# Bias and residual of an output chunk added by one VectorE instruction out of PSUM, in place of a ScalarE copy and a GpSimd addition

## What is computed

```python
q = split_heads(x @ Wq.T)
k, v = split_heads(text @ Wk.T), split_heads(text @ Wv.T)
k_ip, v_ip = split_heads(ip @ Wk_ip.T), split_heads(ip @ Wv_ip.T)
out = merge_heads(attend(q, k, v)) + merge_heads(attend(q, k_ip, v_ip))
return (out @ Wo.T + bo) + x
```

## Time and profile before

| | us |
|---|---|
| median of 3 runs | 683.67 (683.13 to 684.17) |
| the profiled execution | 683.04 |
| its span, first to last instruction | 681.2 |

### The profile page before, as it was taken

One profiled execution on the slowest core, in us unless ns is written; L12 is line 12 of the kernel. 1 busy time (PEld: TensorE's weight loads), 2 busy tenths in 40 slices (PEclk: granted clock), 3 DMA queues, 4 the chain that ended last, 5 costly groups with the idle time before them and its releaser, 6 DMA issues.

```text
span 681.2 us, 18904 instructions
## 1 busy us (share of the span) xinstructions
PE 657.5 (97%) x6514; PEld 564.5 (83%) x6514; DVE 435.7 (64%) x956; ACT 493.3 (72%) x1078; POOL 225.0 (33%) x261
## 2 busy tenths in 40 slices
PE   9959798999999999999999999999999999999997
PEld 9959576788888888888888888888888888888877
DVE  6786677675757566675756576665657566756633
ACT  3983787877868777877777787778777777876730
POOL 4020102243432434343434324343434243342333
PEclk9989898999999999999999999999999999999999
DMA  8950111223131221313131312213131323212212
GB/s 318 410 234 9 25 56 34 80 57 96 49 103 51 82 63 55 93 48 97 51 93 49 99 55 86 55 55 93 48 101 51 90 55 93 56 50 64 56 42 69
DMA packets 34691, 57.46 MB, mean 84 GB/s; under 512 B 4832, under 2 KB 27232, under 8 KB 34400
## 3 DMA queue, kind: packets, MB, share of 16 engines
q1 hardware_dynamic: 34656, 56.99, 27.3%
HBM read 35.34 MB, written 10.49 MB: 67 GB/s over the span
## 4 chain that ended last, share of the span: by engine, by line
PE 85%; DVE 6%; ACT 6%; issue 2%; POOL 0%; DVEq 0%; ACTq 0%
PE q_ps L711 19%; PE x_ps L711 19%; PE sum_ps L769 11%; PE b_ps L752 10%; PE pv_ps L780 10%; PE a_ps L735 7%; PE x_ps L789 5%; PE a_ps L741 1%; ACT probs L405 1%; DVE k_stack L631 1%; DVE k_stack L641 1%; ACT k_stack L485 1%; ACT q_stack L397 1%; DVE wo_lo L554 1%; DVE k_stack L545 1%
## 5 line engine op out<-in xcount | busy, mean ns | idle before, releaser
L405 ACT ACTIVATE probs<-b_ps 77x512 f32<-77x512 f32 x320 | 181.1, 591 | 121.0 <-PE b_ps L752 119.3
L562 DVE TENSOR_TENSOR q_stack<-q_ps,q_hi 32x256 fp32r<-32x256 f32 x320 | 134.3, 420 | 36.0 <-ACT q_hi L390 32.3
L571 DVE TENSOR_REDUCE row_max<-a_ps 128x4 f32<-128x308 f32 x320 | 137.6, 471 | 24.0 <-PE a_ps L735 21.3
L397 ACT ACTIVATE q_stack<-q_hi 32x256 fp32r<-32x256 f32 x320 | 133.0, 416 | 10.0
L598 DVE TENSOR_TENSOR scaled<-x_ps,pv_sb 128x512 f32<-128x512 f32 x75 | 51.9, 692 | 105.4 <-PE x_ps L789 105.0
L752 PE MATMUL b_ps<-q_stack,k_stack 98*77 98x256 f32 x640 | 115.1, 281 | 0.5 <-ACT probs L405 0.5
L347 POOL TENSOR_TENSOR scaled<-scaled 128x256 f32<-128x256 f32 x80 | 59.2, 740 | 139.1 <-DVE scaled L598 139.0
L352 POOL TENSOR_TENSOR attn_lo<-scaled,attn_hi 128x256 fp32r<-128x256 f32 x80 | 59.1, 739 | 113.2 <-ACT attn_hi L434 113.2
L358 POOL TENSOR_TENSOR res<-y,res 128x256 f32<-128x256 f32 x70 | 51.1, 731 | 136.8 <-ACT y L428 136.8
L735 PE MATMUL a_ps<-k_diag,q_hi 128*128 128x308 f32 x320 | 87.3, 313 | 7.0 <-DVE row_max L571 6.8
L752 PEld LDWEIGHTS b_ps<-q_stack,k_stack 98*77 98x77 f32 x640 | 85.7, 146 | 1.5 <-ACT probs L405 1.0
(11 more groups left out here) (111 smaller groups left out, 962.3 us busy)
## 6 DMA issues: line engine op xcount, KB each, us to landing
x_raw<-x_in SPq DMA_DIRECT2D x16, 640.0 KB, 4.2
q_stack<-q_stack SPq DMA_DIRECT2D x80, 128.0 KB, 2.3
res<-x_in SPq DMA_DIRECT2D x75, 128.0 KB, 2.0
y_out<-res SPq DMA_DIRECT2D x75, 128.0 KB, 1.7
stage<-wk_in SPq DMA_DIRECT2D x6, 640.0 KB, 7.9
stage<-wv_in SPq DMA_DIRECT2D x6, 640.0 KB, 10.7
wq_raw<-wq_in SPq DMA_DIRECT2D x1, 1600.0 KB, 10.2
wo_raw<-wo_in SPq DMA_DIRECT2D x1, 1600.0 KB, 14.6
```

The lines of the kernel that those rows point to most:

```text
L397: done = nc.scalar.activation(q_stack[0:D, u.slot, j, :], q_hi[j * D:(j + 1) * D, u.slot, :].bitcast(F32), ACT.Copy)
L405: nc.scalar.activation(probs[0:KEYS, j, :], b_ps[j % 2][0:KEYS, :], ACT.Exp).then_inc(b_drained, 1)
L562: done = nc.vector.tensor_tensor(q_stack[D:2 * D, u.slot, j, :], q_ps[rows, 0:N], q_hi[rows, u.slot, :].bitcast(F32), ALU.subtract)
L571: nc.vector.tensor_reduce(row_max[:, u.slot, br, :, sub], bank[:, 0:BLK].rearrange("p (j n) -> p j n", j=GROUP), AXIS.X, ALU.max).then_inc ...
```

## The change

The ScalarE copy `add_bias` with its buffer `y`, the GpSimd addition `add_residual` and the semaphore `y_added` are taken out. DVE gets a function `finish`, one `scalar_tensor_tensor` that reads the chunk out of `x_ps`, adds the bias as a scalar of each partition and the residual, and writes `res`. It signals `y_done`, for which PE's `spread_inverse` and now SP's `store` wait. In DVE's `emit` it stands behind `q_low`.

```diff
-        y = sbuf("y", [P, 2, N])
...
-        y_added = sem("y_added")
...
             def store(c):
-                wait(sp, y_added, c.number(1, 1))
+                wait(sp, y_done, c.number(1, 1))
...
-            def add_residual(c):
-                wait(pool, y_done, c.number(1, 1))
-                wait(pool, res_loaded[c.g], c.tile(DMA, DMA))
-                nc.gpsimd.tensor_tensor(res[:, c.g, :], y[:, c.slot, :], res[:, c.g, :], ALU.add).then_inc(y_added, 1)
...
-                if chunk.exists():
-                    add_residual(chunk)
...
-            def add_bias(c):
-                wait(act, out_ready, c.number(1, 1))
-                nc.scalar.activation(y[:, c.slot, :], x_ps[:, 0:N], ACT.Identity, bias=bo[:, c.g:c.g + 1]).then_inc(y_done, 1)
...
-                if chunk.exists():
-                    add_bias(chunk)
...
+            def finish(c):
+                wait(dve, out_ready, c.number(1, 1))
+                wait(dve, res_loaded[c.g], c.tile(DMA, DMA))
+                nc.vector.scalar_tensor_tensor(out=res[:, c.g, :], in0=x_ps[:, 0:N], scalar=bo[:, c.g:c.g + 1],
+                                               in1=res[:, c.g, :], op0=ALU.add, op1=ALU.add).then_inc(y_done, 1)
...
                 if u.plus(2).exists():
                     q_low(u.plus(2))
+                if chunk.exists():
+                    finish(chunk)
```

More of the change, by code:

```diff
@@ L353, in attn_low @@
                                         attn_hi[:, u.batch, u.g, :].bitcast(F32), ALU.subtract).then_inc(attn_lo_done, 1)
-            def add_residual(c):
-                wait(pool, y_done, c.number(1, 1))
-                wait(pool, res_loaded[c.g], c.tile(DMA, DMA))
-                nc.gpsimd.tensor_tensor(res[:, c.g, :], y[:, c.slot, :], res[:, c.g, :], ALU.add).then_inc(y_added, 1)
             def emit(u):
-                ahead, norm, chunk = u.tile_plus(1), u.plus(-1 - SPREAD_LAG), u.plus(-OUT_LAG)
+                ahead, norm = u.tile_plus(1), u.plus(-1 - SPREAD_LAG)
                 if norm.exists():
@@ L437, in emit @@
                 before, ahead, nxt = u.tile_plus(-1), u.tile_plus(2), u.plus(2)
-                norm, chunk = u.plus(-1 - SPREAD_LAG), u.plus(-OUT_LAG)
+                norm = u.plus(-1 - SPREAD_LAG)
                 exp(u, 0)
@@ L610, in emit @@
             def emit(u):
-                norm, nxt = u.plus(-1 - SPREAD_LAG), u.plus(1)
+                norm, nxt, chunk = u.plus(-1 - SPREAD_LAG), u.plus(1), u.plus(-OUT_LAG)
                 if norm.exists():
```

## The result

The changed kernel takes 703.45 us (median of 4 runs, 703.13 to 703.65) against 683.89 us: a ratio of 1.0287, 95% interval 1.027 to 1.0305, so 2.9% slower. Its profiled execution took 703.35 us with a span of 701.5 us.

What follows compares the result with a forecast made beforehand. PE's in-order queue was taken to bound the kernel. 14 tile-first stalls of net 1.33 us add 18.6 us to 683.04, giving 701.6, or 702.3 us as a median; the range was 699 to 718 us.

Steps and rivals of the forecast that it cites:

- What bounds the kernel: Middle of the kernel, 142.5 to 629.0 us: PE's own queue sets the pace; work off ScalarE and GpSimd buys nothing.
- The ordinary unit, cost nothing: In 56 of 70 units finish releases x_ps 0.52 us before PE's load at 344.75, so the edit costs nothing.
- The stall of 1.44 us: First unit of a tile: PE's spread waits for q_low's end and finish, 0.88 + 0.03 + 0.48 + 0.05 us.
- 0.11 us given back: After a tile's first spread, the present loss from the multiplication held up by q_low disappears; net 1.33 us.
- 14 times: The stall comes in 14 tile-first units (10, 15, ... 75), of 16 reciprocals; 14 x 1.33 = 18.6 us.
- The sum: Whole kernel: profiled 683.04 us + 18.6 = 701.6; forecast for a median 702.3 us (+2.7%).
- SyncE: Store queue: the store waits for finish, 331.2 instead of 329.93 in tile-first units; loads and copies behind it cost nothing.
- The clock: Rival at the 14 stalls: PE's clock falls, 1.7 us each; 726 us if all, 714 if half; chance 0.25.
- the two rows that pointed opposite ways: At the stall, load row 1.85 us sided with a clock fall, matmul row 1.36 us with none.
- Stalls in ordinary units: Rival: finish over 0.52 us late stalls the other 56 units; 0.2 us beyond gives 713 us; chance 0.05.
- The other side, relief that pays: Rival: ScalarE's exponentials set the pace, 0.47 us less per unit gains 14 us, 669 us; chance 0.04.

## Why the prediction was right, step by step

*What bounds the kernel.* Right. PE's queue sets the pace; 56 chunks moved off ScalarE and GpSimd gave a ratio of 0.9992.

*The ordinary unit, cost nothing.* Right, and the cover was 0.52 us as worked out, or a little more: one more instruction (0.40 us) fits, two (0.80) leave a stall of 0.2 us, which puts it near 0.6.

*The stall of 1.44 us.* Right. q_low ends at 338.45, the new instruction runs from 338.48 to 338.96, PE's load starts at 339.02: 0.03, 0.48 and 0.06 us, where 0.03, 0.48 and 0.05 stood in the sum. The spacing in front of a tile's first spread is 8.90 us in the mean of 14 against 7.44 before, 1.46 us more.

*0.11 us given back.* 0.09: the spacing behind that spread is 7.47 in the mean, 7.56 before. Net 1.37 us and not 1.33.

*14 times.* Right, by the waits. 14 x 1.37 = 19.2 us, where the prediction had 18.6.

*The sum.* The profiled executions are 20.3 us apart. The 1.1 us beyond 19.2 lie ahead of the first stall. This is the spread of unit 9, which has no output chunk, in the kernel before and in the changed one:

```profile
135.47 0.30 PEld L789 LDWEIGHTS x_ps<-inv_parts,spread 128*128 128x128 f32 x2 [0.41 <-issue]
```

```profile
136.54 0.30 PEld L781 LDWEIGHTS x_ps<-inv_parts,spread 128*128 128x128 f32 x2 [0.41 <-issue]
```

Nothing of the change runs before it, and in nine of the traces, whose kernels are alike in what runs up to it, this spread comes anywhere from 135.47 to 137.03. So it is scatter of the start, and the kernel before has the earliest of the nine. The medians are 19.56 us apart; 702.3 was forecast and 703.45 came.

*SyncE.* Right: the store is issued at 338.99, as soon as the new instruction has ended, and no wait for a residual shows up.

*The rivals.* The clock did not fall in 14 stalls of 1.39 us. Of the two rows that pointed opposite ways, the matmul row gave the right answer: the weight-load gap of 1.90 us is longer than the 1.86 us of the earlier trace rows and was harmless. But the prediction read one gap and one fall as if the first decided the second, and the same gap brought none in three of ten traces. That part rested on thin evidence, and its outcome was in part luck; a chance of 0.25, and not none, was the right form for it. The rival's mechanism and price (1.7 us forecast, 1.5 measured) were right, and the margin to it was small. Stalls in ordinary units did not come. The other side, relief that pays, is refuted twice.

## What to carry to other kernels

When a read-out is moved to another engine, look at what stands ahead of it in that engine's queue in every kind of unit, not in the commonest one: four units in five were free, and the fifth paid for all. Compare the moment at which the new place can finish with the moment at which the bank's next user is ready, and add up only the excess. And a long instruction that runs once per tile is worth cutting or moving into an idle stretch before anything is added behind it.

## What the runs showed of the hardware

A VectorE copy of 128x256 fp32 from SBUF to SBUF took 0.66 to 0.74 us in 11 of 16 cases, each time with a GpSimd subtraction running that it outlasted by 0.15 us, and 0.27 at its shortest (line 568 of the kernel without the reciprocal, ns):

```profile
L568 DVE COPY inv<-inv x16: 271/656/736, 108.1 to 662.2; 128x256 f32<-128x256 f32 x16
```

In three of the five short cases such a subtraction began at nearly the same time, and the cast behind the copy (line 571) was the one held up: 0.65 to 0.72 us in place of 0.29, again until 0.15 us after GpSimd's end. q_low and row_max, which read PSUM, do not show this: in this kernel they take 412 to 430 and 465 to 480 ns. The Trainium skill, page "GPSIMD Engine Reference", section "8. Key points", says that the two engines share their SBUF interfaces and contend for VectorE instructions in a two-port mode or with two SBUF inputs. This copy has one SBUF input, so it falls under that sentence only if it ran in a two-port mode, which no view here shows; the section gives no price.

In the first units of tiles TensorE's clock fell oftener the longer PE's matmul row had been idle, with no sharp edge between: not after 1.39 us, after 4 of 14 waits of 1.79 us, after 13 of 14 of 2.18 us. At another place, on the way into the loop, it fell after 7 of 10 gaps of 1.66 us.

Back to back, without a wait between them, the new form starts every 0.40 us (0.39 to 0.40 in all 210 cases of the four kernels that have more of it); the row's 0.48 us is the way to its completion. It is the 0.48 that PE waits for, and the 0.40 that VectorE's queue pays.
